# GpSimd's rotary addition in two instructions of 512 columns instead of one of 1024

## The chip, the cores and the metric

The program runs on one core of a Trainium2 chip. The metric is the device time of one execution in microseconds (us), as the median over several runs. Inside the core five engines work beside each other, each through its own list of instructions in order: TensorE (PE; its weight loads are shown as PEld), VectorE (DVE), ScalarE (ACT), GpSimd (POOL) and SyncE (SP), which here only issues DMA transfers. They wait for each other through semaphores.

## The reference, cut to what matters

The input is 16 sequences of 256 tokens with 128 channels, all in fp32. A first attention block with its own normalisation (called the first block below) is applied once. Then come six layers of local attention and a gated feed-forward network; this is where nearly all the time goes. What matters here is the beginning of each layer:

```python
def attn_layer(x, Wqkv, qs, ksc, Wo):
    q, k, v = jnp.split(x @ Wqkv, 3, -1)          # 16 heads of 64
    q = l2norm(q) * qs
    k = l2norm(k) * ksc
    q = q * cos * scale + rotate_half(q) * sin * scale
    k = k * cos * inv + rotate_half(k) * sin * inv
    out = local_attention(q, k, v)                # windows of 32, each sees itself and the one before
    return out @ Wo
for i in range(6):
    x = attn_layer(shift_tokens(x), Wqkv[i], ...) + x
    x = ffn_layer(shift_tokens(x), ...) + x       # layer norm, W1, a * gelu(gate), W2
```

The rotary step makes of each half of q and k (32 of a head's 64 channels) a sum of two products: one half times a cosine table, the other half times a sine table.

## The kernel before

Channels lie on the 128 partitions and tokens along the columns. One *batch* is one sequence in one layer: six layers of 16 make 96 batches, and they follow each other in one software pipeline. Every engine has a written order of steps for one batch (`PE_ORDER`, `DVE_ORDER`, `ACT_ORDER`, `POOL_ORDER`, `SP_ORDER`). The function `batch` walks through such an order; steps in the list `AHEAD` work for the next batch (projections, rotary step, norms, moves), those in `BEHIND` for the one before (output projection and feed-forward), the rest for the batch itself (scores, softmax, values). Fourteen batches of a layer are written out one after the other, and a loop runs over the layers. Nothing reorders the steps at run time: an engine that waits in one step holds up all its later steps.

The steps that the change and the prediction touch, in the order in which a batch meets them:

- `PA`, `PB` (PE, L1086): projections of k (parts p = 0, 1) and q (p = 2, 3), 512 columns each, into one of two ring banks of PSUM.
- `RA`, `RB` (DVE, L862): each multiplies a bank with two tables, in two instructions of 512 columns, into `prod_a` and `prod_b`. They wait until the addition that last read this half of `prod` is done (L859).
- `AD0` to `AD3` (POOL, L556): the addition `prod_a + prod_b`, 1024 columns in one instruction, into `ks` (p = 0, 1) or `qs` (p = 2, 3). The destination has two rows of 512 columns, for the two halves of the channels. `AD` is the step that the change edits. Between `AD2` and `AD3` stands `RK` (L526 to L534): four small instructions that split the norms of k in bf16 parts.
- `QA`, `QB` (ACT, L638): squares of the same banks, after which a bank is free. `NK`, `NQ` (PE, L1097) sum the squares.
- `M0`, `M1` (DVE): the maxima of the scores, two reductions (L895) of a PSUM bank each and then one small instruction at L900: `neg_max = -row_max * rq`, 16 columns. Both of its inputs, `row_max` and `rq`, lie in SBUF. `M0` stands in `DVE_ORDER` right behind `RA0 RB0` of the next batch and in front of `RA1 RB1`; `M1` stands between `H0` and `H1 H2` (L950), after which comes `UC` (L871).
- `E00` to `E03`, `E10` to `E13` (ACT, L683): the exponentials, with `neg_max` as their bias. ACT's order runs `E00 QA1 QB1 E01 E02 SQ QA2 QB2 LN E03`.
- `S00`, `S01`, `S10`, `S11` (PE, L1141 and L1151): the scores. `S10` starts with a mask product (L1141) into the bank that `E03` has to have read.
- `SQ`, `LN`, `XG`, `VAR`, `UP0`: the layer norm and the first product of the feed-forward network of the batch before.
- `MQ`, `MK`, `MV` (SP, L426 and L437): DMAs that bring q, k and v into the layout of the scores. `MQ` waits for all four additions (`rot_ready`), then `MK` and `MV` follow on the same queue. `S00` of the next batch waits for `MQ` and `MK`.

GpSimd's instruction reads and writes SBUF only. Of DVE's instructions in a batch, L900 is the one with two inputs in SBUF; the others that run beside an addition take one input from PSUM.

Of the kernel before, what the change touches and what calls it, by code (L numbers as in the profile page):

```python
# [9 lines left out]
ALU = mybir.AluOpType  # L10
# [79 lines left out]
def rank(order, s, *kinds):  # L90

    return [x for x in order if x[0] in kinds].index(s)
# [6 lines left out]
def build(nc, t):  # L99

    with ExitStack() as ctx:
# [3 lines left out]
        def sem(name):  # L105
            return ctx.enter_context(nc.semaphore(name))
# [43 lines left out]
        prod_a, prod_b = ([prod[:, i, a, :, :] for i in range(2)] for a in range(2))  # L150
# [46 lines left out]
        def carve(parts, *shape):  # L197
# [11 lines left out]
            if len(shape) == 3:  # L209
# [66 lines left out]
        xs_ready, proj_ready, prod_ready, sq_ready, rot_ready, v_made, v_even_ready, v_odd_ready = (  # L276
            sem(n) for n in ("xs_ready", "proj_ready", "prod_ready", "sq_ready", "rot_ready", "v_made",
                             "v_even_ready", "v_odd_ready"))
# [19 lines left out]
        def at(g, per_batch, n=0):  # L298

            return g * per_batch + (CREDIT + n)  # L300

        def start_with_credit(eng, *sems):
            for s in sems:
                eng.sem_inc(s, CREDIT)

        def moved(g, n=0, moves=MOVES):

            return (g + n) * (16 * moves)
# [13 lines left out]
        def walk(eng, order, step):  # L322

            def middle(g0):
                for b in range(1, BATCH - 1):
                    batch(order, step, g0 + b, b, b % 2)

            for s in order:
                if stage(s) == 1:
                    step(s, 0, 0, 0, 0)  # L330
            step(("LL",), 0, 0, 0, 0)
            batch(order, step, 0, 0, 0, behind=False)
            step(("B1",), 0, 0, 0, 0)
            with eng.Fori(0, DEPTH - 1) as layer:
                g0 = layer * BATCH
                middle(g0)
                batch(order, step, g0 + (BATCH - 1), BATCH - 1, 1, b_ahead=0, new_layer=layer + 1)
                step(("LL",), g0 + BATCH, 0, 0, layer + 1)
                batch(order, step, g0 + BATCH, 0, 0, b_behind=BATCH - 1)
                step(("B1",), g0 + BATCH, 0, 0, layer + 1)  # L340
            g0 = (DEPTH - 1) * BATCH
            middle(g0)
            batch(order, step, g0 + (BATCH - 1), BATCH - 1, 1, ahead=False)
            for s in order:
                if stage(s) == -1:
                    step(s, g0 + (BATCH - 1), BATCH - 1, 1, None)
# [15 lines left out]
        def first_block(eng, body):  # L362


            body(-1, True, False, False)
            body(0, True, True, False)
            with eng.Fori(0, BATCH - 2) as x:
                body(x + 1, True, True, True)
            body(BATCH - 1, False, True, True)
            body(BATCH, False, False, True)  # L370
# [5 lines left out]
        def columns(b):  # L376
            return bass.ds(b * TOKENS, TOKENS)
# [9 lines left out]
        def alone(eng):  # L387


            eng.sem_inc(gates_passed, 1)  # L390
# [107 lines left out]
        @block.gpsimd  # L498
        def _(pool):
            start_with_credit(pool, l_kept, p_kept, rk_parts, rot_ready, tables_ready)  # L500
            pool.memset(xs[:, :], 0.0)
            pool.memset(xs1[:, :], 0.0)
            pool.memset(mean_ones[:, :], 1.0 / DIM)
            pool.memset(ones_col[:, :], 1.0)
            pool.memset(kt[:, :, 0:WINDOW], 0.0).then_inc(memset_done, 1)

            def first_body(i, first, attend, second):
                if first:
                    pool.wait_ge(l_x0, at(i + 1, 1, 1))
                    alone(pool)  # L510
                    pool.tensor_copy(x_all[:, columns(i + 1)], pair_x[:, 0:TOKENS]).then_inc(l_kept, 1)
                if attend:
                    pool.wait_ge(p_x1, at(i, 1, 1))
                    alone(pool)
                    pool.tensor_copy(x1_all[:, columns(i)], pair_x[:, TOKENS:2 * TOKENS]).then_inc(p_kept, 1)

            first_block(pool, first_body)

            def step(s, g, b, parity, layer):
                kind = s[0]  # L520
                if kind == "RK":

                    pool.wait_ge(norms_ready, at(g, 2, 1))
                    pool.wait_ge(rk_turned, at(g, 1))
                    alone(pool)
                    pool.tensor_copy(rk_bf[:, :, 0, :], rk[:, :, :]).then_inc(rk_parts, 1)  # L526
                    pool.wait_ge(rk_parts, at(g, 4, 1))
                    pool.tensor_tensor(rk_rest[:, :, :], rk[:, :, :], rk_bf[:, :, 0, :], ALU.subtract
                                       ).then_inc(rk_parts, 1)
                    pool.wait_ge(rk_parts, at(g, 4, 2))  # L530
                    alone(pool)
                    pool.tensor_copy(rk_bf[:, :, 1, :], rk_rest[:, :, :]).then_inc(rk_parts, 1)
                    pool.wait_ge(rk_parts, at(g, 4, 3))
                    pool.tensor_tensor(rk_bf[:, :, 2, :], rk_rest[:, :, :], rk_bf[:, :, 1, :], ALU.subtract  # L534
                                       ).then_inc(rk_parts, 1)
                if kind == "AD":
                    p = s[1]
                    n, c = p // COUPLES, p % COUPLES
                    if p == 0 and layer is not None:

                        pool.wait_ge(scales_landed, layer * 16 + 16)
                        pool.wait_ge(prod_ready, at(g, QK_BANKS))
                        alone(pool)
                        for m in range(2):
                            for a in range(2):
                                col = qk_scales[:, 2 * m + a:2 * m + a + 1]
                                pool.tensor_scalar(tables[:, m, a, a, :], rotary[:, m, 0, :], col, None, ALU.mult)
                                last = pool.tensor_scalar(tables[:, m, a, 1 - a, :], rotary[:, m, 1, :], col,
                                                          -1.0 if a else 1.0, ALU.mult, ALU.mult)
                        last.then_inc(tables_ready, 1)  # L550
                    last_product = max(rank(DVE_ORDER, (h, p), "RA", "RB") for h in ("RA", "RB"))
                    pool.wait_ge(prod_ready, at(g, QK_BANKS, last_product + 1))
                    if c == 0 and not (isinstance(g, int) and g == 0):
                        pool.wait_ge((k_moved, q_moved)[n], moved(g))
                    dst = (ks, qs)[n][:, :, 2 * c:2 * c + 2, :].rearrange("p a u c -> p a (u c)")
                    pool.tensor_tensor(dst, prod_a[p % 2], prod_b[p % 2], ALU.add  # L556
                                       ).then_inc(rot_ready, 1)

            walk(pool, POOL_ORDER, step)


# [748 lines left out]
```

## Time and profile before

| | |
|---|---|
| Time, median of 3 runs | 4101.15 us (4100.27 to 4104.68) |
| The profiled execution | 4102.04 us, of which the span of the instructions is 4100.3 us |
| PE busy | 3667.7 us (89%), PEld 2551.7 us (62%) |
| DVE busy | 2749.2 us (67%) |
| ACT busy | 2765.6 us (67%) |
| POOL busy | 1037.5 us (25%), 857 instructions |
| Mean granted clock of TensorE | 0.945 of full speed |

The table is the first part of the profile page. Shares are over the whole span; a low share does not say that an engine is off the path that sets the end. The views used below are: the chain of waits (the work that ended last, followed back), the list of waits (who waited for whom), the groups of instructions by line (busy time, mean length, idle time before them), and the timeline (instructions in order of time: start, length, engine, line, operation, and in brackets the idle time before it and what ended it). An `x4` in a timeline means four instructions merged in one row; "issue" is idle time for which the profile shows no waiting.

### The profile page before, as it was taken

The page shows a single profiled execution, that of the slowest core. Times are in us where ns is not written, and L with a number is a line of the kernel's source. Part 1 is how long each engine was busy: PE and PEld are TensorE (multiplying, and loading weights), DVE is VectorE, ACT ScalarE, POOL GpSimd, SP SyncE. Part 2 cuts the span into 40 slices and gives each one's busy share as a digit, 9 for nine tenths or more (in the row PEclk, how much of TensorE's full clock was granted, in tenths as well). Part 3 has the DMA queues.
Part 4 walks back from the last instruction along what each step waited for, and adds up shares of the span by engine and source line. Part 5 has one row for each costly group of instructions (what it writes and reads, how often), then busy time and mean ns, then how long its engine had stood idle before and what let it go on. Part 6 is the DMA issues. An engine that isn't in the chain of part 4 may idle for free.

```text
span 4100.3 us, 162501 instructions
## 1 busy us (share of the span) xinstructions
PE 3667.7 (89%) x64569; PEld 2551.7 (62%) x64761; DVE 2749.2 (67%) x5376; ACT 2765.6 (67%) x9073; POOL 1037.5 (25%) x857
## 2 busy tenths in 40 slices
PE   6777999998899997899997899997899998899997
PEld 3333666665666665666665666665666665666665
DVE  3334777776677776677776677776677776677774
ACT  3443777776677776677776677776677776677775
POOL 0002222322222322223323223322223323233221
PEclk9656999999999999999999999999999999999998
DMA  0002544454544454545454545454544454544543
GB/s 22 6 22 50 119 113 114 106 118 98 130 112 113 109 116 97 128 110 114 107 120 97 126 109 114 109 122 97 126 111 112 110 122 97 119 105 111 120 106 79
DMA packets 367878, 422.12 MB, mean 103 GB/s; under 512 B 58840, under 2 KB 272360, under 8 KB 366360
## 3 DMA queue, kind: packets, MB, share of 16 engines
q1 hardware_dynamic: 367128, 411.67, 43.5%
q8 instruction: 525, 8.60, 1.0%
q14 instruction: 225, 1.84, 0.1%
HBM read 19.30 MB, written 2.10 MB: 5 GB/s over the span
## 4 chain that ended last, share of the span: by engine, by line
PE 77%; issue 4%; ACT 4%; SPq 4%; DVE 1%; DMA 1%; POOL 1%; DVEq 0%; POOLq 0%; ACTq 0%
PE ring_ps L1086 16%; PE ring_ps L1133 8%; PE out_ps L1200 8%; PE out_ps L1188 7%; PE out_ps L1228 7%; PE score_ps L1151 7%; PE turn_ps L1170 5%; PE turn_ps L1162 5%; PE small_ps L1097 4%; PE turn_ps L1235 3%; ACT probs L683 2%; PE score_ps L1141 2%; SPq L426 2%; PE ring_ps L1122 1%; ACT att_t L671 1%
## 5 line engine op out<-in xcount | busy, mean ns | idle before, releaser
L683 ACT ACTIVATE probs<-score_ps,neg_max,rq 128x64 f32<-128x64 f32 x3072 | 1191.9, 418 | 199.1 <-DVE neg_max L900 197.9
L862 DVE TENSOR_TENSOR prod<-ring_ps,tables 128x512 f32<-128x512 f32 x1536 | 952.2, 681 | 262.9 <-PE ring_ps L1086 154.0
L556 POOL TENSOR_TENSOR ks<-prod 128x1024 f32<-128x1024 f32 x192 | 451.7, 2353 | 2068.1 <-DVE prod L862 1895.3
L1086 PE MATMUL ring_ps<-xs,wqk 128*128 128x256 f32 x3072 | 791.9, 397 | 118.7 <-DMA wqk<-in_L_ffn_Wqkv 72.8
L638 ACT ACTIVATE square<-ring_ps,biases 128x512 f32<-128x512 f32 x768 | 508.9, 693 | 384.5 <-DVE prod L862 370.4
L1086 PEld LDWEIGHTS ring_ps<-xs,wqk 128*128 128x128 f32 x3072 | 570.2, 196 | 225.9 <-DMA wqk<-in_L_ffn_Wqkv 74.0
L683 ACT ACTIVATION_READ_ACCUMULATOR probs<-score_ps,neg_max,rq 128x1 f32 x3072 | 673.8, 219 | 0.0
L671 ACT ACTIVATE att_t<-turn_ps 128x512 f32<-128x512 f32 x384 | 229.3, 597 | 462.5 <-PE turn_ps L1170 462.5
L556 POOL TENSOR_TENSOR qs<-prod 128x1024 f32<-128x1024 f32 x192 | 451.9, 2354 | 236.1 <-DVE prod L862 224.2
L1133 PE MATMUL ring_ps<-wv,xs 128*128 128x512 f32 x768 | 402.3, 627 | 12.8 <-issue 12.8
L1188 PE MATMUL out_ps<-v,pt 64*32 64x64 f32 x24576 | 345.7, 224 | 62.7 <-issue 56.1
L1188 PEld LDWEIGHTS out_ps<-v,pt 64*32 64x32 f32 x24576 | 277.1, 105 | 150.9 <-issue 149.1
L1200 PE MATMUL out_ps<-att_t,wo 128*128 128x256 f32 x1536 | 350.4, 381 | 0.7 <-ACT att_t L671 0.7
L917 DVE TENSOR_TENSOR att<-out_ps,inv_sums 128x512 f32<-128x512 f32 x384 | 247.4, 686 | 131.6 <-PE out_ps L1188 128.3
L1151 PEld LDWEIGHTS score_ps<-kt,qt 64*32 64x32 f32 x24576 | 264.4, 106 | 114.2 <-issue 113.8
L1151 PE MATMUL score_ps<-kt,qt 64*32 64x64 f32 x24576 | 299.7, 228 | 26.3 <-DMA kt<-ks 14.1
L1200 PEld LDWEIGHTS out_ps<-att_t,wo 128*128 128x128 f32 x1536 | 294.6, 192 | 41.9 <-ACT att_t L671 0.9
L1170 PEld LDWEIGHTS turn_ps<-ident,att 128*128 128x128 f32 x1536 | 175.1, 144 | 222.3 <-ACT att_t L671 148.8
L1170 PE MATMUL turn_ps<-ident,att 128*128 128x128 f32 x1536 | 252.2, 288 | 68.0 <-ACT att_t L671 66.7
L907 DVE COPY pt<-turn_ps 128x512 f32<-128x512 f32 x384 | 262.6, 684 | 74.6 <-PE turn_ps L1162 73.9
L1228 PE MATMUL out_ps<-xg,w 128*128 128x256 f32 (+1 forms) x1152 | 302.2, 398 | 3.9 <-DVE xg L943 3.2
L895 DVE TENSOR_REDUCE row_max<-score_ps 128x8 f32<-128x512 f32 x384 | 246.4, 683 | 77.2 <-PE score_ps L1151 77.2
(156 smaller groups left out, 4512.2 us busy)
## 6 DMA issues: line engine op xcount, KB each, us to landing
v<-vs SPq DMA_DIRECT2D x1344, 128.0 KB
qt<-qs SPq DMA_DIRECT2D x768, 128.0 KB
kt<-ks SPq DMA_DIRECT2D x768, 128.0 KB
v<-vs SPq DMA_DIRECT2D x192, 64.0 KB
wqk<-in_L_ffn_Wqkv SPq DMA_DIRECT2D x6, 1024.0 KB, 5.1
wv<-in_L_ffn_Wqkv SPq DMA_DIRECT2D x6, 512.0 KB, 5.3
wo<-in_L_ffn_Wo SPq DMA_DIRECT2D x6, 512.0 KB
prod<-in_L_attn_x SPq DMA_DIRECT2D x16, 128.0 KB, 2.1
```

The costliest lines, as they stand in the source:

```text
L556: pool.tensor_tensor(dst, prod_a[p % 2], prod_b[p % 2], ALU.add).then_inc(rot_ready, 1)
L638: nc.scalar.activation(square[p % COUPLES][a][:, :], bank_of(("PB" if a else "PA", p), parity)[:, :], ACT.Square, bias=zero_col[:, :]).the ...
L671: nc.scalar.activation(att_t[:, 4 * c:4 * c + 4, P * i:P * (i + 1)], turn_ps[:, :].rearrange("p (j c) -> p j c", c=P), ACT.Copy).then_inc( ...
L683: last = nc.scalar.activation(probs[i][:, j, e, :], score_ps[e][:, KEYS * j:KEYS * (j + 1)], ACT.Exp, bias=neg_max[:, h:h + 1], scale=rq[p ...
L862: last = V.tensor_tensor((prod_b if a else prod_a)[p % 2][:, f, :] .rearrange("p (u c) -> p u c", u=2), bank[:, :].rearrange("p (u c) -> p ...
L1086: last = mm(bank_of(s, parity)[:, TOKENS * f:TOKENS * (f + 1)], wqk[:, n, 2 * c + f, a, :], xs[:, WINDOW:PADDED], start=True, stop=True)
L1133: mm(bank_of(s, parity)[:, :], xs[:, WINDOW + P * i:WINDOW + P * (i + 1)], heads[:, :, e, :], start=True, stop=True).then_inc(v_made, 1)
L1151: last = mm(score_ps[e][WINDOW * w:WINDOW * (w + 1), KEYS * j:KEYS * (j + 1)], qt[64 * e:64 * e + 64, j, q0:q0 + WINDOW], kt[64 * e:64 * e ...
L1170: last = pe.transpose(turn_ps[:, P * j:P * (j + 1)], att[i][:, 4 * c + j, :, :].rearrange("p e k -> p (e k)"), ident[:, :])
L1188: last = mm(out_ps[e][WINDOW * w:WINDOW * (w + 1), DIM_HEAD * j:DIM_HEAD * (j + 1)], pt[64 * e:64 * e + 64, j, WINDOW * w:WINDOW * (w + 1) ...
L1200: last = mm(out_ps[0][:, 0:TOKENS], wo[:, j, :], att_t[:, j, :], start=(j == 0), stop=(j == PAIRS - 1))
L1228: last = mm(out_ps[c % 2][0:size, TOKENS * n:TOKENS * (n + 1)], w1[:, col:col + size], xg[:, :], start=True, stop=True)
```

## The change

One instruction of `AD` becomes two, one for each row of the destination. Only the second of them increments the semaphore `rot_ready`. The waits before the step, the data and the order stay as they are.

```diff
                     dst = (ks, qs)[n][:, :, 2 * c:2 * c + 2, :].rearrange("p a u c -> p a (u c)")
-                    pool.tensor_tensor(dst, prod_a[p % 2], prod_b[p % 2], ALU.add
-                                       ).then_inc(rot_ready, 1)
+                    for f in range(2):
+                        last = pool.tensor_tensor(dst[:, f, :], prod_a[p % 2][:, f, :], prod_b[p % 2][:, f, :], ALU.add)
+                    last.then_inc(rot_ready, 1)
```

## Rows read from the trace of the kernel before

**Rows 1.** Page, chain that ended last by engine; list of waits: us, times, longest.

```profile
PE 77%; issue 4%; ACT 4%; SPq 4%; DVE 1%; DMA 1%; POOL 1%; DVEq 0%; POOLq 0%; ACTq 0%
...
ACT probs L683 <- DVE neg_max L900: 197.9, 97, 6.3
...
PE out_ps L1188 <- issue: 56.1, 83, 2.3
```

**Rows 2.** Timeline, one batch from AD0 on: start us, length us, engine, line.

```profile
2066.33 2.35 POOL L556 TENSOR_TENSOR ks<-prod 128x1024 f32<-128x1024 f32 x1 [18.38 <-DVE prod L862]
...
2067.98 0.73 DVE L900 SCALAR_TENSOR_TENSOR neg_max<-row_max,rq 128x16 f32<-128x16 f32 x1
...
2068.74 0.40 ACT L683 ACTIVATE probs<-score_ps,neg_max,rq 128x64 f32<-128x64 f32 x1 [1.86 <-DVE neg_max L900]
...
2071.14 0.69 ACT L638 ACTIVATE square<-ring_ps,biases 128x512 f32<-128x512 f32 x1 [0.16 <-DVE prod L862]
...
2073.90 1.07 PE L1097 MATMUL small_ps<-square,head_ones 128*32 128x256 f32 x16
...
2075.13 1.31 ACT L638 ACTIVATE square<-ring_ps,biases 128x512 f32<-128x512 f32 x2
...
2078.68 0.20 ACT L683 ACTIVATION_READ_ACCUMULATOR probs<-score_ps,neg_max,rq 128x1 f32 x1
...
2078.94 0.16 PEld L1141 LDWEIGHTS score_ps<-mask_bf,ident_bf 128*128 128x128 bf16 x2 [0.18 <-ACT probs L683]
```

**Rows 3.** Timeline, first and last of 58 such batches, GpSimd's AD0.

```profile
470.04 2.35 POOL L556 TENSOR_TENSOR ks<-prod 128x1024 f32<-128x1024 f32 x1 [19.48 <-DVE prod L862]
...
3999.88 2.35 POOL L556 TENSOR_TENSOR ks<-prod 128x1024 f32<-128x1024 f32 x1 [20.03 <-DVE prod L862]
```

**Rows 4.** Timeline, L900 in the two batches of rows 3, VectorE.

```profile
471.70 0.71 DVE L900 SCALAR_TENSOR_TENSOR neg_max<-row_max,rq 128x16 f32<-128x16 f32 x1
...
4001.61 0.66 DVE L900 SCALAR_TENSOR_TENSOR neg_max<-row_max,rq 128x16 f32<-128x16 f32 x1
```

**Rows 5.** Timeline, a batch with a late S01: L900, and ACT's later wait.

```profile
760.41 0.18 DVE L900 SCALAR_TENSOR_TENSOR neg_max<-row_max,rq 128x16 f32<-128x16 f32 x1
...
767.65 1.26 ACT L638 ACTIVATE square<-ring_ps,biases 128x512 f32<-128x512 f32 x2 [0.41 <-PE small_ps L1097]
```

**Rows 6.** Timeline, the last batch of a layer (one of five), VectorE's L900.

```profile
3430.56 1.32 DVE L900 SCALAR_TENSOR_TENSOR neg_max<-row_max,rq 128x16 f32<-128x16 f32 x1
```

**Rows 7.** Groups by line, GpSimd: busy us, mean ns, idle before.

```profile
L556 POOL TENSOR_TENSOR ks<-prod 128x1024 f32<-128x1024 f32 x192 | 451.7, 2353 | 2068.1 <-DVE prod L862 1895.3 <-DMA kt<-ks 132.9 <-issue 39.9
L528 POOL TENSOR_TENSOR rk_rest<-rk,rk_bf 128x32 f32<-128x32 f32 x96 | 23.5, 245 | 7.7
```

**Rows 8.** Timeline, GpSimd, two instructions back to back without a wait.

```profile
3422.12 0.48 POOL L548 TENSOR_SCALAR tables<-rotary,qk_scales 128x256 f32<-128x256 f32 x1
3422.58 0.92 POOL L547 TENSOR_SCALAR tables<-rotary,qk_scales 128x256 f32<-128x256 f32 x1
```

**Rows 9.** Timeline, the same batch as rows 2, around AD3 and M1.

```profile
2079.66 0.21 POOL L526 CAST rk_bf<-rk 128x32 bf16<-128x32 f32 x1 [1.68 <-ACT rk L660]
...
2081.04 2.35 POOL L556 TENSOR_TENSOR qs<-prod 128x1024 f32<-128x1024 f32 x1
...
2082.95 0.48 DVE L900 SCALAR_TENSOR_TENSOR neg_max<-row_max,rq 128x16 f32<-128x16 f32 x1
...
2083.46 1.28 ACT L665 ACT_TABLE_LOAD   x1
...
2084.14 0.27 DVE L871 COPY rkt<-ring_ps 48x256 bf16<-48x256 bf16 x1
...
2084.67 0.11 PEld L1122 LDWEIGHTS ring_ps<-rkt,head_sel_bf 48*128 48x128 bf16 x2 [0.41 <-issue]
```

**Rows 10.** Timeline, the moves of k, and the scores that wait for them.

```profile
2054.72 6.05 SPq L426 DMA_DIRECT2D kt<-ks  x8
...
2064.87 1.41 PEld L1151 LDWEIGHTS score_ps<-kt,qt 64*32 64x32 f32 x128 [0.42 <-issue]
```

## Prediction

> **What bounds the kernel now.** I began with the chain that ended last: TensorE has 77% of it and GpSimd 1% [rows 1]. So what GpSimd takes longer counts only where somebody waits for it, and I looked for that in the list of waits. GpSimd hardly appears there as the one waited for, but one wait leads to it: ScalarE waits 97 times, once in a batch, for `neg_max` of L900, 197.9 us together [rows 1]. The timeline of a batch shows why L900 is late. It starts at 2067.98 and takes 0.73 us for 16 columns [rows 2]. In another batch the same instruction takes 0.18 [rows 5]. The difference is AD0: it runs from 2066.33 to 2068.68, and L900 ends at 2068.71. Two more batches show it again: AD0 ends at 472.39 and L900 at 472.41; AD0 at 4002.23 and L900 at 4002.27 [rows 3, 4]. I went through all 192 of L900: 178 overlap an addition, and these end some 0.03 us behind it (at most 0.17); the other 14 take about 0.18. So L900 does not run while a GpSimd addition runs: it waits for the addition's end. Its two inputs lie in SBUF, and so do the addition's; the other DVE instructions of the batch, one input of which comes from PSUM, run beside an addition without this.
>
> What hangs on that end is the way of the batch to `S10`. E00 starts at 2068.74, right behind L900; RA1 and RB1 stand behind L900 on VectorE, and QB1 waits for RB1 (0.16 idle); after that ACT has no gap that a wait explains until E03 is read out at 2078.88, and at 2078.94 PE loads the weights of `S10`, released by ACT [rows 2]. How much room is beside it? NK on PE ends at 2074.97, and QA2, which needs it, starts at 2075.13 [rows 2]. Where S01 came late and L900 was not held up, it was QA2 that waited for NK, 0.41 us [rows 5]. So PE's own way is only some 0.1 to 0.2 us shorter than the way through AD0, L900 and ACT: an earlier L900 wins hardly anything, and a later one costs in full.
>
> **The change, part by part.** *What an addition costs in two parts.* One of 1024 columns takes 2.353 us; the nearest two-input addition on GpSimd, 32 columns, takes 0.245 [rows 7]. That is (2.353 - 0.245) / 992 = 2.125 ns for a column and 0.177 us fixed. A half is then 0.177 + 512 x 0.002125 = 1.265 us. Back to back, without a wait, the next instruction started 0.02 us before the one before it ended (0.48 long, 0.46 apart) [rows 8]. A pair is 2 x 1.265 - 0.02 = 2.51 us: 0.157 us more than one. Bounds by the same rows: if all of the 0.245 were fixed, the surplus would be 0.245 - 0.02 = 0.225. The 32 columns and the 1024 both have an operand of two rows; if the fixed 0.177 came from the second row alone, halves would have none of it and the pair would be 0.177 shorter. I take 0.157, since an instruction's start is likelier to cost than its second row, and keep -0.18 and +0.225 as ends.
>
> By the Trainium skill's GPSIMD Engine Reference, section 3.1, the same addition over 2048 columns takes 4497 ns; as an estimate from that and the 2353 ns here, the slope is 2.09 ns, the surplus 0.19 us, and the sum below would be 12 us instead of 9.9. No run here has 2048 columns.
>
> *Where L900 of M0 then stands.* It starts 1.65 us after AD0 began (2067.98 - 2066.33) [rows 2]; in the batches where it is held up it is 1.38 to 1.91 mostly. The first half is over at 1.27. So L900 meets the second half, and waits for its end, 0.157 later than now. I count 58 batches like this one (the first and the last are [rows 3, 4]), in which ACT has no gap from E00 to E03 beyond the 0.16 before QB1, which moves along. There PE's S10 comes later by the surplus: 58 x 0.157 = 9.1 us. In 20 more the hold is there, but ACT waits later for something else, as the 0.41 of [rows 5]: nothing, or a few hundredths. In 13 L900 is free. In 5, the last of a layer each, L900 comes 1.06 us after the start, inside the first half, and waits 1.32 in all [rows 6]; if nothing gets between the halves, 5 x 0.157 = 0.8. Sum 9.9.
>
> *What takes some of it back.* Behind S10 PE loses 56.1 us in 83 gaps at L1188 for which no wait is shown [rows 1]. A batch that arrives later may find such a gap shorter. The ends are nothing and all of it in 83 of 96 batches (8.6 us); no row shows which. I take off 1.2 and keep both ends.
>
> *M1 and the rest.* L900 of M1 is held up by AD3 in the same way, to 2083.43 [rows 9]. Behind it, E10 needs ACT's table load first, which ends at 2084.74, so 0.157 is covered by 1.3 us. UC ends at 2084.41 and KN0's weights follow at 2084.67: 0.26, of which one sequencer step (0.12 at the least in any batch) is needed: covered, just; at the upper end it would be 0.1 us in a batch. AD1 and AD2 are read much later, and RK behind AD2 has 1.68 us of idle time before it [rows 9]. AD3 moves the start of MQ, MK and MV, which are behind each other on SP's queue: 0.157 later each. MK is issued by 2060.77 and S00 needs it at 2064.87 [rows 10]; the landing takes under 2 us where S00 does wait for it, so 2 us are left (1 us in the tightest ordinary batch). The cover is the PE work between, and if it were gone each batch would pay 0.157. At a layer's first batch MQ stands behind the late weights' DMAs, not behind AD3. Only in the very first batch does S00 wait on AD3: 0.16. GpSimd gets one more instruction per addition, 384 in all, with 75% of its time idle.
>
> **The sum.** 9.9 + 0.16 - 1.2 = 8.9 us on the profiled 4102.04 gives 4110.9. The profiled execution is 0.9 above the median of the runs (4101.15), so the forecast is 4110.
>
> **Rivals.**
>
> *Nothing to be seen.* The surplus is smaller than 0.157 (the 0.177 partly hidden under the first half), or the gaps at L1188 take most of it back. For it: the engine sequence on PE has such gaps in most batches. Against: in the 58 batches the time from S00 to S10 is the same to about a tenth (14.5 to 14.7 us), so little is slack there. With half the surplus or two thirds of the sum taken back: 4101 to 4106.
>
> *Not slower: VectorE gets in between the halves.* If the first half ended after L900's start, or the second half let L900 pass, L900 would end about 0.5 us earlier [rows 2]. It decides at 1.65 us against a first half of 1.27; only the 5 last batches of a layer (1.06) are on the other side now [rows 6]. The price is bounded by PE's own way: 0.1 us in 58 batches and some 0.3 in 5, together 7.3 us, so 4094; a pair shorter by 0.18 ends in the same place, 4095 to 4097. For it: GpSimd's hold is then given up once in the middle. Against: the start at 1.65 in nearly every batch.
> The Trainium skill's "SBUF — State Buffer", section "SBUF: two separate sides", says that a VectorE instruction with two SBUF inputs and a GpSimd instruction take their shared ports as a lock for the whole instruction, whoever starts first. By that rule two short holds would serve VectorE sooner wherever it is already waiting when the first ends: here in the 5 last batches of a layer, but not in the 58. That L900 ends 0.03 us behind AD0 agrees with it; that two instructions leave a way in between them is shown by no row of before.
>
> *Dearer halves.* The surplus is at the upper end or over it: 0.225 x 63 = 14.2 us, and KN0's cover is used up: 4115 to 4121. For it: another GpSimd instruction of 256 columns takes 0.92 us where its neighbour takes 0.48 [rows 8], so the form can matter more than the columns. Against: nothing in the form of a half is new but its length.
>
> **How the numbers follow.** Forecast (L900 held longer, 4107 to 4113) 0.42, nothing to be seen 0.36, not slower 0.10, dearer 0.12. What the measurement tells from no change is 0.2%, that is 8.2 us: slower means above 4109.4, faster below 4093. Of the forecast's 0.42 I put 0.35 above the line and 0.07 within it; dearer adds 0.12 and a little of "nothing" goes with it: slower 0.48. Of "not slower" 0.06 is faster. The rest, 0.46, is within. The range leaves out the farthest part of the dearer halves and of the gain: 4097 to 4117.
>
> **What would show it.** In the profile after: L556 in 768 instructions of about 1.27 us, pairs of 2.5 us with no gap; L900 of M0 ending 0.03 us behind the second half, at about 0.89 us instead of 0.73; E00 to S10 as long as now, S00 to S10 longer by the surplus in the 58 batches; the waits of S00 for the moves of k unchanged in number. L900 ending in the middle of a pair would show the second rival, halves of 1.3 and more the third, and an S00 to S10 that is longer with a batch that is not, the first. The prediction is wrong if the pair takes no longer, or if L900 is no longer held up.

## The result, and the profile after

| | before | after |
|---|---|---|
| Time, median of 6 runs each on one chip | 4101.81 us (4100.27 to 4106.2) | 4123.76 us (4114.35 to 4131.49) |
| Ratio, 95% interval | | 1.0049 [1.0036, 1.0062] |
| The profiled execution | 4102.04 us, span 4100.3 us | 4131.49 us, span 4129.7 us |
| POOL busy | 1037.5 us, 857 instructions | 1091.7 us, 1241 instructions |
| Mean granted clock of TensorE | 0.945 | 0.941 |

On a second chip the ratio was 1.0045 [1.003, 1.006] (4114.81 against 4097.03 us). By these ratios the change costs 20 and 18 us, 12 to 25 by the intervals (the medians differ by 22 and 18). Forecast were 9, to 4110, with a range up to 4117. The direction was right, the time was outside the range. The profiled execution after is the slowest of its six; another one, on the second chip, took 4116.72.

The first view is the page of after and its groups by line, GpSimd's addition. It answers to [rows 7].

```profile
PE 3678.6 (89%) x64569; PEld 2555.4 (62%) x64761; DVE 2765.6 (67%) x5376; ACT 2765.9 (67%) x9073; POOL 1091.7 (26%) x1241
...
L557 POOL TENSOR_TENSOR ks<-prod 128x512 f32<-128x512 f32 x384 | 478.8, 1268 | 2070.1 <-DVE prod L863 1877.4 <-DMA kt<-ks 135.3 <-issue 57.4
```

A half takes 1.268 us (1.265 were worked out).

The second view is the timeline of after, the same batch as [rows 2] (start, length; `x2` merges the two halves).

```profile
2082.30 2.50 POOL L557 TENSOR_TENSOR ks<-prod 128x512 f32<-128x512 f32 x2 [18.24 <-DVE prod L863]
...
2083.97 0.86 DVE L901 SCALAR_TENSOR_TENSOR neg_max<-row_max,rq 128x16 f32<-128x16 f32 x1
...
2084.87 0.40 ACT L684 ACTIVATE probs<-score_ps,neg_max,rq 128x64 f32<-128x64 f32 x1 [2.01 <-DVE neg_max L901]
...
2087.26 0.69 ACT L639 ACTIVATE square<-ring_ps,biases 128x512 f32<-128x512 f32 x1 [0.16 <-DVE prod L863]
...
2095.06 0.16 PEld L1142 LDWEIGHTS score_ps<-mask_bf,ident_bf 128*128 128x128 bf16 x2 [0.18 <-ACT probs L684]
```

S00's mask weights of the same batch, the start of the step to S10, before and after:

```profile
2064.13 0.31 PEld L1141 LDWEIGHTS score_ps<-mask_bf,ident_bf 128*128 128x128 bf16 x2
```

```profile
2080.10 0.31 PEld L1142 LDWEIGHTS score_ps<-mask_bf,ident_bf 128*128 128x128 bf16 x2
```

The pair ends at 2084.80 and L901 (L900 of before) at 2084.83: 0.03 behind it, 0.86 long instead of 0.73. E00 to S10's weights take 10.19 us, and took 10.20. So what lies between L901 and S10 is shifted by the surplus of the pair and by nothing else. Over all batches the median from S00's mask weights to S10's goes from 14.81 to 14.95 us.

The third view is the same timeline around AD3 and M1, to be laid beside [rows 9].

```profile
2097.16 2.49 POOL L557 TENSOR_TENSOR qs<-prod 128x512 f32<-128x512 f32 x2
...
2099.07 0.61 DVE L901 SCALAR_TENSOR_TENSOR neg_max<-row_max,rq 128x16 f32<-128x16 f32 x1
...
2099.61 0.86 DVE L951 SCALAR_TENSOR_TENSOR hidden<-out_ps,b_full,gate 128x256 f32<-128x256 f32 x2
...
2100.39 0.27 DVE L872 COPY rkt<-ring_ps 48x256 bf16<-48x256 bf16 x1
...
2100.88 0.12 PEld L1123 LDWEIGHTS ring_ps<-rkt,head_sel_bf 48*128 48x128 bf16 x2 [0.50 <-issue]
...
2101.32 0.72 PEld L1189 LDWEIGHTS out_ps<-v,pt 64*32 64x32 f32 x64 [0.32 <-issue]
```

PV00's weights of the same batch before:

```profile
2085.07 0.72 PEld L1188 LDWEIGHTS out_ps<-v,pt 64*32 64x32 f32 x64 [0.29 <-issue]
```

Here is the second place. Behind L901 come H1 and H2 (L951), then UC (L872), and KN0's weights (L1123) wait for UC. PV00, the first product of the values, is PE's next step. KN0 now starts 0.22 us after UC's end; before it was 0.26, with 0.41 of idle time ahead of it, now 0.50. The view calls this idle time "issue", waiting for nothing that it shows, in both kernels. That it is a wait shows when KN0's start is laid against UC's end in all batches. Before: median 0.262 in 95 batches. After: 0.213, under 0.22 in 74 of the batches and under 0.208 in none. From S10's weights to KN0's the median goes from 5.73 to 5.82 us, and from there to PV00's (L1189) from 0.40 to 0.45. The list of waits sums it: the idle time ahead of KN0's and KN1's weights, first before, then after (us, times, longest).

```profile
PEld ring_ps L1122 <- issue: 71.6, 190, 0.8
```

```profile
ACT probs L684 <- DVE neg_max L901: 206.1, 96, 6.3
...
PEld ring_ps L1123 <- issue: 79.0, 190, 0.8
...
PE out_ps L1189 <- issue: 62.9, 91, 2.4
```

What fills this gap is in the trace, among the instructions of TensorE's sequencer, which the timeline leaves out: short ones that work out a count or wait for a semaphore. In the 80 batches that the loop over the layers runs, before and after alike, the first of them starts 0.04 us behind UC's end, a second follows, then KN0's weights may go, then four more, then PV00's; from one to the next it takes some 0.1 us (0.095 to 0.149, medians). So PV00 comes 0.66 us behind UC's end (median) in both kernels: it had nothing to spare before the change either, whereas KN0, which also has PE's work before it, had 0.05 us. From S10 to PV00 the median goes from 6.13 to 6.27 us, the whole surplus of 0.14. Thirteen of the last layer's batches, which are written out behind the loop and have fewer such instructions there, stay as they were.

Lastly the timeline of after in the last batch of a layer, which answers to [rows 6].

```profile
2213.78 2.50 POOL L557 TENSOR_TENSOR ks<-prod 128x512 f32<-128x512 f32 x2 [2.85 <-DVE prod L863]
2214.85 0.24 DVE L901 SCALAR_TENSOR_TENSOR neg_max<-row_max,rq 128x16 f32<-128x16 f32 x1
2215.12 0.40 ACT L684 ACTIVATE probs<-score_ps,neg_max,rq 128x64 f32<-128x64 f32 x1 [0.78 <-DVE neg_max L901]
```

L901 begins 1.07 us into the pair and ends 1.31 into it, right behind the first half and 1.19 ahead of the pair's end. So it got in at the halves' boundary and did not wait for the second, in all five batches of this kind.

**The sum of after.** The batches' ways from S00 to S10 are 11 us longer in all. Of these, 8.1 us come from 58 batches that grew by 0.1 to 0.2 us; the other 3 lie in batches that differ as much between two executions of the kernel before (3.7 us). The ways from S10 to PV00 are 10 us longer, 7 of them up to KN0, and 9.7 of the 10 come from 69 batches that grew by some 0.14. Together that is 21 of the 29.45 us between the two profiled executions; the change's own part of it is 8 + 10 = 18, close to the 18 to 20 of the ratios. The other 8 us lie behind PV00, among them the gaps at L1189 (56.1 us before, 62.9 here, 59.1 in the profile of the second chip); they differ from one execution to the next. The lower granted clock (0.941 against 0.945) doesn't explain them: of 30 executions of the kernel before on a third chip, the 12 at 0.940 or less took 4102.5 us in the mean, the 11 at 0.944 or more 4104.2.

### The profile page after: what moved, and what is told of

The parts are those of the page before. It is cut to its first block, busy times and chain, and to the rows that moved or that the text cites. A ratio compares the mean times of both kernels' runs of the same rounds, so it can differ in the third digit from the quotient of the medians.

```text
span 4129.7 us, 162885 instructions
## 1 busy us (share of the span) xinstructions
PE 3678.6 (89%) x64569; PEld 2555.4 (62%) x64761; DVE 2765.6 (67%) x5376; ACT 2765.9 (67%) x9073; POOL 1091.7 (26%) x1241
## 4 chain that ended last, share of the span: by engine, by line
PE 77%; issue 4%; ACT 4%; SPq 4%; DMA 1%; DVE 1%; POOL 1%; DVEq 0%; ACTq 0%; POOLq 0%
PE ring_ps L1087 17%; PE out_ps L1201 8%; PE ring_ps L1134 8%; PE out_ps L1189 7%; PE out_ps L1229 7%; PE score_ps L1152 7%; PE turn_ps L1171 5%; PE turn_ps L1163 4%; PE small_ps L1098 4%; PE turn_ps L1236 3%; ACT probs L684 2%; PE score_ps L1142 2%; SPq L426 2%; PE ring_ps L1123 1%; ACT att_t L672 1%
## 5 line engine op out<-in xcount | busy, mean ns | idle before, releaser
L557 POOL TENSOR_TENSOR ks<-prod 128x512 f32<-128x512 f32 x384 | 478.8, 1268 | 2070.1 <-DVE prod L863 1877.4
L557 POOL TENSOR_TENSOR qs<-prod 128x512 f32<-128x512 f32 x384 | 479.0, 1269 | 219.0 <-DVE prod L863 206.5
L1189 PE MATMUL out_ps<-v,pt 64*32 64x64 f32 x24576 | 345.7, 224 | 72.0 <-issue 62.9
L1189 PEld LDWEIGHTS out_ps<-v,pt 64*32 64x32 f32 x24576 | 277.1, 105 | 162.1 <-issue 159.4
```

The costliest lines, as they stand in the source:

```text
L557: last = pool.tensor_tensor(dst[:, f, :], prod_a[p % 2][:, f, :], prod_b[p % 2][:, f, :], ALU.add)
L1189: last = mm(out_ps[e][WINDOW * w:WINDOW * (w + 1), DIM_HEAD * j:DIM_HEAD * (j + 1)], pt[64 * e:64 * e + 64, j, WINDOW * w:WINDOW * (w + 1) ...
```

## The experiments

The theory: while a GpSimd addition runs, L900 waits for the end of that one *instruction*. The surplus of a pair then counts at two places, AD0 with M0 (S10 late) and AD3 with M1 (UC and KN0 late). The rivals put it elsewhere: in the halves of AD1 and AD2, in a hold over the whole pair, or in a hold of anything that VectorE reads in SBUF. In the expectations that have letters, A is this theory. Differences in us are the ratio's, taken of the median of before; the medians themselves can differ from that by some us. In the diffs, "pair" and "whole" stand for the loop over two halves and for the one instruction.

**One addition at a time.** AD0 alone in halves:

```diff
+                    if p in (0,):
+                        ... pair
+                    else:
+                        ... whole
```

> Only AD0 is split; AD1, AD2, AD3 stay in one instruction. Theory A (two holds of VectorE's L900, one under AD0 and one under AD3, each 0.14 us longer): only the first is left, S00 to S10 longer by 0.14 us in some 60 batches, KN0 as before: +8 to +10 us, about 4111. Rival B (each split addition costs the same wherever it stands, by its additional instruction): a quarter of 22 us, +5.5, about 4107. Rival C (the first hold alone explains all, and the rest is PE's gaps): +20, about 4122.

Measured: ratio 1.0 [0.9985, 1.0015], 4094.82 against 4093.05 us: 0 within 6 us, a miss on the clock. The trace has the step as expected: S00 to S10 at 14.97 us instead of 14.81, S10 to KN0 at 5.73 as before. So it was run again, on another chip:

> AD0 alone in halves, a second time and on another chip. Theory (the step's +0.14 us in 58 batches reaches the end): +8 to +10 us. Rival (the step is later by as much, but PE makes it good further on, as the first run of it had it, ratio 1.000): 0 within 6 us.

Measured: ratio 1.0021 [1.0009, 1.0032], 4112.67 against 4102.65: +8.6 us, 4 to 13. The two executions' steps agree to 0.01 us. The term reaches the end on the second chip; why it didn't on the first no view shows. This interval holds the theory's 8 to 10 us and rival B's 5.5 alike; the steps decide, since only S00 to S10 has moved.

AD3 alone, `if p in (3,)`:

> Only AD3 is split. Theory A: S00 to S10 unchanged, KN0 later by 0.11 us and the values' product behind it by 0.03 in some 88 batches: +10 to +12 us, about 4113. Rival B: +5.5, about 4107. Rival C: nothing, 4102, since AD3 moves only the start of the transfers of q, which have 1 to 2 us to spare.

Measured: ratio 1.0017 [1.0004, 1.003], +7 us, 2 to 12, which holds the theory's and rival B's figure alike. The steps are the theory's: S00 to S10 is unchanged at 14.81; S10 to KN0 is 5.82, KN0 starts 0.214 behind UC's end, and S10 to PV00 is 6.27. The same line of the list of waits, in this kernel:

```profile
PEld ring_ps L1126 <- issue: 79.4, 190, 0.8
```

AD1 and AD2 alone, `if p in (1, 2)`:

> Only AD1 and AD2 are split, under which no instruction with two inputs in SBUF runs on VectorE. Theory A: nothing, 4102 within 3 us. Rival B: half of 22 us, +11, about 4113.

Measured: ratio 0.9983 [0.9971, 0.9995], 7 us faster by the interval, 2 to 12. Rival B's 11 us are ruled out. Neither step has changed (14.82 and 5.73), and the line has its old value:

```profile
PEld ring_ps L1126 <- issue: 71.9, 190, 0.8
```

I have no cause for these 7 us; the medians of the two kernels don't differ (4093.24 against 4093.05). By the ratios all four kernels of this chip (the fourth is the full change with UC early, below) lie 3 to 8 us under what their steps add up to. A reference that came out too long there would do that; no trace of the kernel before was taken on this chip, so it isn't shown. These runs say how far a difference of 0.2% may be taken: single terms are better read from the steps, and the clock settles sums.

AD0 and AD3 together, `if p in (0, 3)`, beside the kernel before once more:

> AD0 and AD3 in halves, AD1 and AD2 whole. Theory (the two places where VectorE's next instruction waits for the end of the pair are all that counts): as the full change, +17 to +20 us against before; mask product's weights 14.95 us after the state's, UC's reader 5.82 us after those. Rival (the two places don't add up to the change; AD1 and AD2 in halves cost something that only shows together with them): +6 to +10 us, the sum of the two single splits on the clock.

> The kernel before, unchanged, for its trace on the same chip as the others of this call. All theories: ratio 1.00 within 0.3%; steps as in the first trace of before, 14.81 us from the state's matmuls to the weights of the mask product and 5.73 us from there to the weights that wait for UC.

Measured: AD0 and AD3 1.0033 [1.0018, 1.0047], +13.5 us, with both steps of the full change (14.96 and 5.82); the kernel before against itself 1.0006 [0.9995, 1.0016], with its steps at 14.82 and 5.73. The two single ones add up to 8.6 + 7 = 15.6. The 18 to 20 of the full change lie at the upper end of this interval (7 to 19) or just over it, and the rival's 6 to 10 partly inside. So the clock doesn't settle it; by the steps, these two places are what the halves cost, and AD1 and AD2 add no loss that could be told.

**The second place undone.** The full change, with UC ahead of H1 and H2 on VectorE:

```diff
-... RB3 RA3 H0 M1 H1 H2 UC TC01 ...
+... RB3 RA3 H0 M1 UC H1 H2 TC01 ...
```

> The changed kernel with one move in VectorE's order: UC (the copy that KN0 waits for) ahead of H1 and H2, right behind M1. UC then ends some 0.6 us earlier. Theory A: KN0 no longer waits for UC, so the second term goes, S00 to S10 stays 0.14 us longer: 10 to 12 us less than the changed kernel, about 4112. Rival (KN0's later start is only where PE's delay shows, its cause lies elsewhere): as the changed kernel, 4122 to 4124.

Measured: ratio 0.9985 [0.9972, 0.9998], 4087.76 us: 6 us *faster* than before, although AD0's term is there (14.96). KN0 now comes 0.897 us behind UC's end and S10 to KN0 is 5.73. The expectation was a gain of 10 to 12 us on the change, and this is some 25. From S10 to PV00 the batches take 18 us less than with the change, where they had lost 10: the other 8 were lost before the change already, since from KN0's weights to PV00's it takes 0.32 us here (median), but 0.40 before. The remaining 7 us are in neither step.

Timeline of this kernel, the same batch:

```profile
2068.00 0.27 DVE L872 COPY rkt<-ring_ps 48x256 bf16<-48x256 bf16 x1
...
2069.16 0.11 PEld L1123 LDWEIGHTS ring_ps<-rkt,head_sel_bf 48*128 48x128 bf16 x2 [0.41 <-issue]
...
2069.49 0.61 PEld L1189 LDWEIGHTS out_ps<-v,pt 64*32 64x32 f32 x56 [0.21 <-issue]
```

UC being early, TensorE's sequencer is done with all six of its instructions before KN0's weights go, and PV00 waits for PE's own work alone. So a UC that ends 0.26 us ahead of KN0 already made the step behind KN0 wait 0.08 us, 8 us over all batches: there was no cover to lose. H2 and TC01, which stand beside UC on VectorE, aren't what PV00 waits for: here H2 ends 0.34 us later behind S10 than before, and TC01 ends after PV00 has begun (medians).

**Smaller parts.** Each addition in four instructions of 256 columns:

```diff
+                    for f in range(2):
+                        for h in range(2):
+                            cut = slice(256 * h, 256 * (h + 1))
+                            ... dst[:, f, cut], prod_a[p % 2][:, f, cut], prod_b[p % 2][:, f, cut]
```

> Every addition in four instructions of 256 columns, about 0.72 us each, 2.8 us together. Theory A with the port given up at each end of an instruction: L900 starts 1.65 us (M0) or 1.91 us (M1) after the first of them, in the third, and gets in at 2.12, so it ends 0.1 us EARLIER than in the kernel before: S00 to S10 shorter by 0 to 0.1 us, KN0 not later: -8 to 0 us against the kernel before. Rival B (surplus counts by the number of instructions): three times the changed kernel's, +50 to +66. Rival E (VectorE waits until GpSimd has nothing more in its queue): L900 ends at 2.8, 0.45 later: +60 to +80.

Measured beside a repeat of the change:

> The changed kernel once more, unchanged, beside the kernel before on the chip of these runs. Theory A (two holds): 0.14 us in some 60 batches and 0.11 to 0.14 in some 88: +17 to +22 us. Rival D (the batches' terms are there, but PE's unexplained gaps take most of them back, as the sum of the runs with one or two additions split suggests, 0, +7 and -7): +0 to +8 us.

The change: 1.0045, as told above. Four parts: 0.996 [0.9947, 0.9973], 4080.3 against 4097.03 us, 16 us faster than before, although the four take 2.78 us together. That is more than the 0 to 8 us expected: S00 to S10 is 14.75, as expected, but the expectation left out that KN0 to PV00 goes from 0.40 to 0.32, 8 us in all. Its timeline, the same batch:

```profile
2053.04 2.78 POOL L559 TENSOR_TENSOR ks<-prod 128x256 f32<-128x256 f32 x4 [17.95 <-DVE prod L866]
...
2054.73 0.43 DVE L904 SCALAR_TENSOR_TENSOR neg_max<-row_max,rq 128x16 f32<-128x16 f32 x1
2055.20 0.40 ACT L687 ACTIVATE probs<-score_ps,neg_max,rq 128x64 f32<-128x64 f32 x1 [1.60 <-DVE neg_max L904]
...
2067.64 2.78 POOL L559 TENSOR_TENSOR qs<-prod 128x256 f32<-128x256 f32 x4
...
2069.55 0.21 DVE L904 SCALAR_TENSOR_TENSOR neg_max<-row_max,rq 128x16 f32<-128x16 f32 x1
...
2070.52 0.27 DVE L875 COPY rkt<-ring_ps 48x256 bf16<-48x256 bf16 x1
...
2071.27 0.11 PEld L1126 LDWEIGHTS ring_ps<-rkt,head_sel_bf 48*128 48x128 bf16 x2 [0.41 <-issue]
```

L904 starts 1.69 us into AD0, inside the third part, and ends 2.12 into it, before the fourth is done (2.78). In 172 of the 192 it ends so at a boundary inside the four, in 162 of these 0.66 us ahead of the whole's end. The hold is that of one instruction, and a waiting VectorE is served between two of GpSimd's that stand back to back. This is the strongest of the experiments: the same edit, carried further, changes its sign, since now a boundary lies between L904's start and the end of the whole.

The Trainium skill, "SBUF — State Buffer", section "SBUF: two separate sides", has the shared ports as an exclusive lock for a whole instruction, taken by whoever starts first. The five batches and the four parts agree with it.

**The hold taken away.** The full change, with L901 reading PSUM in place of `row_max`, so that only one input lies in SBUF; the kernel leaves out the subtraction of the rows' maxima:

```diff
-... in0=row_max[:, :, :].rearrange("p j e -> p (j e)"), scalar=-1.0, in1=rq[parity][:, i, :] ...
+... in0=score_ps[0][:, 0:HEADS], scalar=0.0, in1=rq[parity][:, i, :] ...
```

> The full change, but M's first instruction reads its 16 columns from PSUM and subtracts 0.0, so that it has one input in SBUF and not two; the subtraction of the maximum is left out. Theory (the hold comes of two inputs in SBUF): M's instruction lasts about 0.2 us in the ordinary batches and ends over 1.5 us before AD0's second half; mask product's weights 14.6 to 14.8 us after the state's, below before; UC's reader still 5.82 us after those; time -10 to +8 us against before. Rival (any VectorE instruction that reads SBUF is held): M's instruction 0.7 us and more, 14.95 us, time as the full change, +15 to +20 us.

Measured: ratio 0.9965 [0.9952, 0.9979], -14 us, where -10 to +8 were expected. Timeline:

```profile
2066.52 2.50 POOL L557 TENSOR_TENSOR ks<-prod 128x512 f32<-128x512 f32 x2 [18.23 <-DVE prod L863]
...
2068.18 0.17 DVE L901 SCALAR_TENSOR_TENSOR neg_max<-score_ps,rq 128x16 f32<-128x16 f32 x1
2068.39 0.41 ACT L684 ACTIVATE probs<-score_ps,neg_max,rq 128x64 f32<-128x64 f32 x1 [1.30 <-DVE neg_max L901]
```

L901 starts 1.66 into the pair and is not held: 0.17 us. S10's weights come after 14.74 us. That a VectorE instruction with one input in SBUF runs beside the addition is now shown with the very instruction. I had expected UC's reader to stay late; it didn't (5.72), since M1's L901 goes free as well, which the expectation forgot.

**Both holds turned to use.** Before, with AD0 waiting until M0's L900 is done; and the same with UC ahead of H1 and H2:

```diff
+                    if p == 0 and not (isinstance(g, int) and g == 0):
+                        pool.wait_ge(nb_ready, at(g - 1, TILES, 1))
```

> The kernel before, additions whole, but AD0 waits until L900 of M0 is done, so that L900 takes 0.18 us and AD0 starts some 1.8 us later; RA2, which needs AD0, has some 4.4 us. Theory A: S00 to S10 shorter by what PE's own way leaves, 0 to 0.1 us in 58 batches, and up to 0.3 in 5: -8 to 0 us. Rival (ACT's way is the only one to S10): 0.55 us in 58 batches, -32. Rival (L900's hold is nothing to the time): within 1.

> The kernel before, additions whole, with AD0 behind M0's L900 and UC ahead of H1 and H2: both places where L900's hold reaches PE are taken off. Theory A: S00 to S10 shorter by 0 to 0.1 us, S10 to KN0 by 0 to 0.05 us: -12 to -3 us against the kernel before. Rival (PE's gaps decide): no difference.

Measured: AD0 behind M0 0.9983 [0.9972, 0.9995], 4089.04 us, -7; with UC early too 0.9941 [0.9928, 0.9953], 4071.16 against 4097.03 us, -24, twice the most that was expected (-12 to -3). The timeline of the latter:

```profile
2050.96 0.17 DVE L902 SCALAR_TENSOR_TENSOR neg_max<-row_max,rq 128x16 f32<-128x16 f32 x1
2051.38 4.69 POOL L558 TENSOR_TENSOR ks<-prod 128x1024 f32<-128x1024 f32 x2 [20.46 <-DVE neg_max L902]
...
2066.21 0.27 DVE L873 COPY rkt<-ring_ps 48x256 bf16<-48x256 bf16 x1
...
2067.53 0.11 PEld L1124 LDWEIGHTS ring_ps<-rkt,head_sel_bf 48*128 48x128 bf16 x2 [0.41 <-issue]
...
2067.85 0.70 PEld L1190 LDWEIGHTS out_ps<-v,pt 64*32 64x32 f32 x64 [0.21 <-issue]
```

AD0 starts behind L902, AD1 follows it without a gap, and L902 takes 0.17 us. Freed from the hold, S10 wins only 0.07 us (14.74 against 14.81): PE's own way is next, a little sooner than the 0.1 to 0.2 that the prediction gave it. UC early is worth 17 us in a kernel without a split; 9 of them lie between S10 and PV00, the rest behind PV00, and no run here says why. This version beats both kernels, by 24 us and 43 us on the same chip.

## Why the prediction was wrong

Point by point:

- *The pair.* 2.50 us instead of 2.51; surplus 0.14, not 0.157. Right.
- *M0's hold.* L901 ends 0.03 behind the second half, 0.86 long (0.89 forecast). With the 5 last batches 9.9 us were forecast for it; the steps show 8 in the 58 batches (58 x 0.14), the clock 0 and 8.6 for AD0 alone. Right in mechanism, and in size as far as it can be told.
- *The 5 last batches of a layer.* I charged 0.8 for "nothing gets between the halves". L901 does get in there. So the mechanism of the rival "Not slower" exists, and decides where it said, by L900's start against the first half's end: for it in 5 batches, against it in the 58.
- *What is taken back.* -1.2 for gaps at L1188 that shrink, a choice between two ends that no row settled. They did not (62.9 and 59.1 us after, 56.1 and 58.6 in two profiles of before).
- *M1 and KN0: the step that failed.* "0.26, of which one sequencer step (0.12 at the least in any batch) is needed: covered, just", and nothing in the sum. By its own figures 0.26 - 0.12 = 0.14 was already less than the surplus of 0.157. And the 0.12 came from one batch, the pipeline's first, which is written out ahead of the loop and has one sequencer instruction between UC and KN0; a batch of the loop has two, and KN0 needs 0.21. So KN0's cover was 0.262 - 0.213 = 0.05 us, and of a surplus of 0.14 the 0.09 is left by which S10 to KN0 grew. PV00 the prediction didn't look at: with four more such instructions it stood 0.66 us behind UC's end already, with no cover at all. So it comes the whole 0.14 later, 10 us over all batches (7 up to KN0, 3 more behind it). This is the missing half: with these 10 us the sum would have been 19, that is 4120.
- *MQ, MK, MV.* S00's waits for the moves of k are 6 before, 14.1 us together, and 6 after, 17.0 us; in second executions 15.7 and 14.9. Covered, as said.
- *AD1, AD2.* No step changed. Right.
- "Dearer halves" had nearly the right time (4115 to 4121) and the right place in it, KN0, but hung it on a surplus of 0.225; in that it was lucky. A surplus of 0.14 was enough. I had the need at 0.12 because I took the smallest of 96 values. The need is what the step takes when it *does* wait: at KN0 hardly any batch showed that before the change, but at PV00 most of the loop's 80 did.

Open stay the 0 us of AD0 alone on its first chip, the 7 us that AD1 and AD2 in halves are faster, some 8 us behind PV00 in the slowest of the executions of after, and what UC early wins behind PV00.

## What to carry to other kernels

Splitting an instruction that holds another engine helps where a boundary falls behind the moment when the other begins to wait, and costs the surplus where it doesn't: two halves lost 18 us, four quarters won 16 (8 of these at PV00), and a wait that lets the short instruction go first won 7 without any split. Cover is measured by the distance between two events when the one does wait for the other, as the median of many such cases; the smallest distance in a trace without that wait comes from another situation, here from a batch outside the loop. It has to be measured at every step that hangs on the wait: KN0 had 0.05 us, PV00 behind it none. A gap that the profile calls "issue" can be a wait that was fulfilled just too late: lay the start against the end of the producer before you call it idle.

## What the runs showed of the hardware

- A VectorE instruction with two inputs in SBUF that meets a GpSimd addition ends 0.03 us behind that instruction's end, and is not made to wait for the next GpSimd instruction, though that stands ready: 5 batches with halves, 172 of 192 with quarters. The GpSimd pair takes 2.50 us in those 5 as in the others. With one input in PSUM it takes 0.17 us beside the addition.
- The addition's cost over its length: 2353 ns for 1024 columns, 1268 for 512, 727 for 256 (back to back, 2.78 us for four of them).
- TensorE's weight load that waits for VectorE's copy comes 0.213 us after the copy's end (median after the change, 0.208 at the least), with two sequencer instructions between; the next step's weights, with four more between, come 0.66 us after it. In the loop's batches a copy that is done 0.26 us ahead of the first therefore still costs 0.08 us in the step behind it (KN0 to PV00 0.40 us); with 0.46, 0.47, 0.9 and 1.05 us it is 0.32. In thirteen of the last layer's batches, outside the loop, 0.23 us ahead was enough for 0.32.
